# A fused GroupNorm and quantised 1x1 convolution: two channels of two conv groups in a partition, products as 64x64 quarters

## The reference, cut to what matters

```
v   = group_norm(x, 32 groups of 16 channels)            # eps 1e-5, no scale
xa  = round(clip((v - lA) / (uA - lA), 0, 1) * 15) / 15   # conv groups rotated: group g reads block g+1 of 4
wq  = (round(clip((w - lW) / (uW - lW), 0, 1) * 15) / 15 - 0.5) * 2
y   = grouped 1x1 conv(xa, wq)                            # 4 groups of 128 channels in, 128 out
y   = relu(y * inv + (beta - running_mean * inv))         # inv = gamma / sqrt(running_var + eps)
out = x + y + v
```

## Time and profile before

| | us |
|---|---|
| runs (three) | 258.25, 258.49, 258.49; median 258.49 |
| profiled execution | 258.41 |
| its span | 256.7 |
| VectorE busy | 230.0 |
| ScalarE busy | 215.2 |
| GpSimd busy | 212.0 |
| TensorE products and averages busy | 193.9 |
| mean granted TensorE clock | 0.902 |

### The profile page before, as it was taken

How to read it: one execution, slowest core, us unless ns; L and a number is a source line. 1 busy time by engine, 2 the same in 40 slices (tenths; PEclk the granted TensorE clock), 3 DMA queues, 4 the chain that set the end, 5 groups by cost and what they waited for, 6 DMA issues and landing times.

```text
span 256.7 us, 3463 instructions
## 1 busy us (share of the span) xinstructions
PE 193.9 (76%) x999; PEld 109.3 (43%) x999; DVE 230.0 (90%) x363; ACT 215.2 (84%) x394; POOL 212.0 (83%) x340
## 2 busy tenths in 40 slices
PE   1142996969889888979797997877696969889920
PEld 0132644435454444445443554343444435454510
DVE  2898698999999999999999899999999999969940
ACT  4437898999999999989999889999899888999300
POOL 6126869999999999999999999999999999999100
PEclk9999999797979798988979599999979797979995
DMA  6999999999999999999999999999999999999994
GB/s 225 398 411 411 408 409 406 418 416 417 418 414 418 417 416 418 411 418 416 416 415 416 418 416 413 419 417 415 417 413 418 416 418 409 402 400 402 393 399 193
DMA packets 34516, 103.25 MB, mean 402 GB/s; under 512 B 1202, under 2 KB 1730, under 8 KB 34498
## 3 DMA queue, kind: packets, MB, share of 16 engines
q1 hardware_dynamic: 18624, 54.86, 53.8%
q10 hardware_dynamic: 15874, 48.18, 47.0%
HBM read 51.65 MB, written 51.38 MB: 401 GB/s over the span
## 4 chain that ended last, share of the span: by engine, by line
POOL 52%; DVE 16%; issue 11%; PE 9%; ACT 5%; DMA 2%; DVEq 0%; SPq 0%; POOLq 0%; ACTq 0%
POOL images L413 27%; POOL levels L424 8%; DVE images L482 7%; PE prod L604 6%; DVE stats L460 4%; POOL dev L375 3%; DVE codes L475 3%; PE var_ps L584 3%; POOL dev L378 2%; DMA images<-in_x 2%; POOL scaled L404 2%; ACT levels L270 2%; POOL coef L406 2%; POOL norm L402 1%; ACT unused L242 1%
## 5 line engine op out<-in xcount | busy, mean ns | idle before, releaser
L604 PE MATMUL prod<-codes,w_t 128*128 128x392 bf16 x768 | 160.8, 369 | 7.9 <-DVE codes L475 2.9
L482 DVE SCALAR_TENSOR_TENSOR images<-prod,floor,images 128x784 f32<-128x784 f32 x128 | 128.0, 1019 | 8.5 <-PE prod L604 8.2
L413 POOL TENSOR_SCALAR images<-images,coef 128x784 f32<-128x784 f32 x120 | 123.7, 1042 | 0.0
L604 PEld LDWEIGHTS prod<-codes,w_t 128*128 128x128 bf16 x768 | 79.1, 110 | 81.6 <-issue 24.6
L270 ACT ACTIVATE levels<-images,coef 128x784 int16<-128x784 f32 x95 | 91.3, 1028 | 1.1 <-issue 1.1
L460 DVE BATCH_NORM_STATS2 stats<-images 128x6 f32<-128x392 f32 x136 | 68.9, 551 | 5.4 <-DMA images<-in_x 5.4
L236 ACT ACTIVATE unused<-images 128x784 bf16<-128x784 f32 x60 | 50.7, 847 | 7.5 <-DMA images<-in_x 5.2
L242 ACT ACTIVATE unused<-images,sums 128x784 bf16<-128x784 f32 x60 | 56.1, 939 | 0.1
L475 DVE TENSOR_SCALAR codes<-levels 128x3136 bf16<-128x3136 int16 x32 | 34.7, 1085 | 1.0 <-ACT levels L270 0.7
L584 PE MATMUL var_ps<-dev,avg 128*128 128x8 f32 x128 | 19.6, 280 | 20.0 <-POOL dev L382 20.0
L424 POOL TENSOR_SCALAR levels<-images,coef 128x784 int16<-128x784 f32 x33 | 33.6, 1020 | 0.1
(11 more groups left out here) (66 smaller groups left out, 83.2 us busy)
## 6 DMA issues: line engine op xcount, KB each, us to landing
images<-in_x SPq DMA_DIRECT2D x30, 1568.0 KB, 14.5
out<-images ACTq DMA_DIRECT2D x30, 1568.0 KB, 18.8
images<-in_x SPq DMA_DIRECT2D x8, 392.0 KB, 6.6
out<-images SPq DMA_DIRECT2D x1, 1568.0 KB, 8.8
out<-images SPq DMA_DIRECT2D x4, 392.0 KB, 7.4
w_raw<-in_weight SPq DMA_DIRECT2D x1, 256.0 KB, 6.5
rows<-in_channel_params ACTq DMA_DIRECT2D x1, 8.0 KB, 2.3
limit_row<-in_limits ACTq DMA_DIRECT2D x1, 0.0 KB
```

Of the source, the lines that this page charges most:

```text
L413: nc.gpsimd.tensor_scalar(here, here, coef[:, u % 2, 0, 1, G * j + o:G * j + o + 1], coef[:, u % 2, 1, 1, G * j + o:G * j + o + 1], ALU.mu ...
L482: nc.vector.scalar_tensor_tensor(out=two, in0=prod[:, k % SETS, :, 0:HALF], scalar=floor[:, o:o + 1], in1=two, op0=ALU.max, op1=ALU.add).t ...
L604: done = nc.tensor.matmul(prod[:, k % SETS, h, 0:HALF], w_t[:, part, output_group(g)], codes[:, n % 2, g, h * HALF:(h + 1) * HALF], start= ...
```

## The change

**Layout.** A partition now holds two neighbouring channels (2i, 2i + 1) of two conv groups: partitions 0 to 63 have blocks 0 and 3, partitions 64 to 127 have blocks 1 and 2. In HBM the two channels are one row of 6272 bytes. Slots 0 and 1 of a partition are the two channels (t = 0, 1) of its first block (y = 0), slots 2 and 3 those of its second (y = 1). Every load and every store becomes two DMAs, one for each half of the partitions; the increments they must reach double. ScalarE issues two DMAs for a store, SyncE two for a load. The four first pieces of images 0 and 1 become two pieces of two slots each, each of two DMAs.

**Products.** An image's 24 products of 128x128 become 96 of 64x64 by 392 columns (L685), four in turn on the four quarters of the array, each with its own weight load. They come as two halves of an image, t = 0 and t = 1, of 48 products that fill two of the three PSUM blocks at once, and `multiplied` rises once for a half. The wait for `final` and for `capped` stands at the start of each half. Ahead of a half, and again ahead of its last four products, stands a new product of the whole array with one column (`after_wait`, L657), which carries the waits for `final` and for the affine step.

**Order of finishing.** VectorE finishes slots in the order 0, 2, 1, 3 (`ORDER`); only F0 and F2 wait for TensorE. F3 now comes straight after F2, and the four halves of statistics stand behind it.

**Norm coefficients.** Both channels of a partition and slot pair are of one norm group, so the small tiles have half the width. The deviations are folded on GpSimd before TensorE's averages: two more GpSimd instructions for a pair (L434, L435), one more wait each. `sums` and the folded tile exist once instead of twice, so `sum_stats` and ScalarE's first sum of a pair now wait for the pair before. TensorE's average of squares moves from behind the means to the deviations.

**TensorE's program** is a loop of two images, run 14 times, with waits against registers, and three images behind it. `HELPED` falls from 4 to 3. At the start VectorE doubles the channel parameters (L556), and TensorE turns them twice.

```diff
+PSUM_SET = ((0, 1, 2, 0), (1, 2, 0, 1))
+ORDER = (0, 2, 1, 3)
+BODY = 2
...
+    LOW, HIGH = slice(0, HP), slice(HP, P)
+    GROUPS = ((LOW, slice(0, G, G - 1)), (HIGH, slice(1, G - 1)))
...
             def load(n):
                 j = n % RING
                 if n >= RING:
-                    sync.wait_ge(stored[j], DMA * (n // RING))
-                sync.dma_start(images[:, j], x_v[n]).then_inc(x_loaded[j], DMA)
...
+                    sync.wait_ge(stored[j], 2 * DMA * (n // RING))
+                for part, groups in GROUPS:
+                    sync.dma_start(pairs_of(images[part, j]),
+                                   x_v[n, groups].rearrange("y i f -> i y f")).then_inc(x_loaded[j], DMA)
...
+                folded(u, 2, nc.gpsimd.tensor_tensor(dev2[:], dev_, dev_, ALU.mult))
+                folded(u, 3, nc.gpsimd.tensor_tensor(dev2_half[:], dev2[:, :, 0:2], dev2[:, :, 2:4], ALU.add))
+                nc.gpsimd.tensor_tensor(dev2_sum[:].rearrange("p j g -> p (j g)"), dev2_half[:, :, 0], dev2_half[:, :, 1],
+                                        ALU.add).then_inc(dev_done, 1)
...
             def finish(n, g):
-                o = output_group(g)
-                k = G * n + g
-                dve.wait_ge(multiplied, k + 1)
+                o = ORDER[g]
+                if g % 2 == 0:
+                    dve.wait_ge(multiplied, 2 * n + g // 2 + 1)
...
                 finish(n, 2)
-                if m < B:
-                    half_stats(m, 0, 0)
                 finish(n, 3)
                 if m < B:
-                    half_stats(m, 0, 1)
-                    half_stats(m, 1, 0)
-                    half_stats(m, 1, 1)
+                    group_stats(m, 0)
+                    group_stats(m, 1)
...
+            def after_wait(out_set, h):
+                nc.tensor.matmul(prod[:, out_set, h, HALF:HALF + 1], w_t[:, 0, 0, 0], w_t[:, 0, 0, 0, 0:1], start=True, stop=True)
...
+            def multiply(trip, i, t):
+                n, sets = BODY * trip + i, PSUM_SET[i % 2][2 * t:2 * t + 2]
+                if t == 0:
                     pe.wait_ge(capped, n + 1)
...
+                if i > 0 or t == 1:
+                    pe.wait_ge(final, G * n + 1 if t == 1 else G * n - i % 2)
+                after_wait(sets[0], 0)
                 for part in range(PARTS):
...
+                    for s in range(2):
+                        for h in range(2):
+                            if (part, s, h) == (PARTS - 1, 1, 1):
+                                wait_affines(n, i, t)
+                                after_wait(sets[0], 0)
+                            for y, inputs in ((0, HIGH), (1, LOW)):
+                                for c, outputs in enumerate((LOW, HIGH)):
+                                    done = nc.tensor.matmul(prod[outputs, sets[y], h, 0:HALF], w_t[inputs, part, t, s, outputs],
+                                                            codes[inputs, i % 2, 2 * c + s, h * HALF:(h + 1) * HALF],
+                                                            start=(part == 0 and s == 0), stop=(part == PARTS - 1 and s == 1))
                 done.then_inc(multiplied, 1)
...
+            with pe.Fori(0, chained_images // BODY) as trip:
+                for i in range(1, 1 + BODY):
+                    image_products(trip, i, True)
```

311 lines of the change are left out of this document (174 added, 137 removed).

## The result

The changed kernel takes 357.3 us (median of four runs, 353.4 to 362.4) against 258.5 us, +99 us. The ratio is 1.358, with a 95% interval from 1.341 to 1.374; it compares fast executions alone (348.4 and 353.4 us, where four others took 357.0 to 364.0 at a lower granted clock), and by it the change costs 92 us, not 99. The direction was forecast, the size was not: +99 us stood against a forecast of +32, and the time lies outside the range of 264 to 335. The profiled execution has a span of 351.7 us, against 256.7.

A forecast was written before the change was run, and what follows sets the result against it. VectorE, ScalarE and GpSimd were taken as nearly full, DMA close behind; VectorE would now wait for TensorE. Last finish 246.9 + 23.6 + 11.9 + 2.0 = 284.4, span 288.8, plus 1.7: 290.5 us against 258.5; range 264 to 335.

The forecast's parts named there:

- T and the windows: T: end of the finish freeing a block to the finish using the half, 2.66 us; VectorE's windows: 1.85, 2.02, 3.04.
- The rivals in which issue binds or quarters run one after another: TensorE's quarter products: T = 6.0, 498 us; chance 0.09, shared with DMA at half rate throughout.
- The rival in which weight loads bind: TensorE's quarter weight loads set the pace: T 3.0 to 3.4, time 308 to 332 us; chance 0.19.
- Term 1: Images 0 to 26, 13.5 pairs: VectorE waits 1.75 us more in each pair for TensorE, +23.6 us.
- term 2: Last five images, 27 to 31, without statistics to fill the windows: 37.0 us instead of 25.1, +11.9.
- I price at 2.4: TensorE's clock: all work priced at 2.4 GHz; 3.6 us at 1.2 in each pair would cost up to +24 us.
- the text's signs of being wrong: F0 and F2 waiting under 10 us in all (mechanism); spacing of a group of four quarters not near 0.17 (T).
- term 5: TensorE's loop: register steps and a branch once a pair fall while TensorE waits for VectorE, 0 us; +14 if uncovered.
- term 3: Start: F0 of image 0 waits for 12 half-clock steps instead of 6; with first loads and parameters, +2.0 us in all.
- Its rival: Start: half-partition loads at half rate put the first F0 at 42.3, not 31: +11.3, time 302 us; chance 0.18.
- Term 4: GpSimd: two folds add 0.6 us to a pair's 13.9, covered by the 15.7 a pair then takes.
- Term 6: End: the last store lands unqueued, so the span ends 0.27 + 3.1 + 1.0 us after the last finish.

The follow-up runs named there:

- e12: e4 plus five unread 392-column products ahead of each half's wait, except at the second half of odd images: 276.3 us, 1.065 of the kernel before.
- e14: Changed kernel, loop written out, five unread products ahead of each half's wait except odd images' second half, and a fourth wait before the averages of means: 311.2 us.
- e4: The kernel before, whole-array products kept but released and awaited by halves of an image, with the changed kernel's waits and finishing order: 296.1 us, 1.141.
- e10: The kernel before with products released in halves of an image and every load and store as two 64-partition transfers: 318.2 us, 1.227.
- e18: e15 plus three more unread products ahead of the wait of the averages of means, loop kept: 312.2 us, 1.210.
- e1: Changed kernel with five unread products ahead of each half's wait from image 1 on, and a fourth wait before the averages of means: 324.8 us, 1.253.
- e8: Changed kernel with each one-column whole-array product issued twice in a row: 357.2 us, 1.369.
- e11: Changed kernel with TensorE's loop of two images written out, waits against constants, no register steps or branch: 325.3 us, 1.254.
- e16: e11 with two unneeded VectorE reductions ahead of each pair's sums, delaying the averages of means: 326.9 us, 1.263.
- e19: e11 with six unneeded VectorE reductions ahead of each pair's sums, delaying the averages of means: 369.8 us.
- e3: The kernel before with each load and store of an image issued as two 64-partition DMAs, nothing else changed: 296.3 us, 1.143.
- e2: Changed kernel with upper-half loads of images 0 to 5 issued from ScalarE's queue, so both partition halves move at once: 353.8 us.
- e15: Changed kernel, loop kept, with five unread products ahead of each half's wait except odd images' second half, and a fourth wait before the averages: 322.9 us.

## Why the prediction was wrong, and where it was right

**T and the windows were right.** At the full clock T is 2.65, against 2.66, and F1 and F3 never wait. Part of that match is luck: the two whole-array products cost 0.11 + 0.22 where 0.40 was forecast, the last group 0.36 where 0.33 was, the hand-overs 0.07 + 0.06 where 0.10 was. A group of four quarters takes (2.02 - 0.36) / 10 = 0.166 us, a row of four alone 0.36. The step from T = 2.26 to 2.66 was about right too: forecast at 19.8 us, and 18.6 from e12 to e14, of which the half transfers may be up to 5 (1.5 + 3.9 from e4 to e10). The rivals in which issue binds or quarters run one after another are out (a quarter every 0.04 us; their sum, by the way, comes to 496, not 498). The rival in which weight loads bind is out: the Trainium skill's "TensorEngine Tiling (Array Packing)", Restrictions, says that tiling by columns switches fast weight load off, but here 48 loads are hidden all the same. So is a price of 0.25 for each whole-array product, which the text took as better if the same page's drain on a change of mode (Key Properties) counts: 0.33 for the two, not 0.50. The mode's part in it no run separates.

**With the clock held up the sum holds, all but the start and the end.** In e18 (312.2 us, clock 0.991) the pair takes 16.2 us, against 14.1 + 1.75 = 15.85; the last five images take 37.3, against 37.0. Term 1 is then 28.0 in place of 23.6, term 2 12.2 in place of 11.9. The first finish comes at 43.72, 12.7 us later than forecast, and from the last finish to the end it is 8.1 us, 3.7 more. Added to the forecast's 290.5 these make the 311.8 us of e18's profiled execution to 0.2. What lies above that, up to 357.3, goes by the clock, as the 33 slow halves against e18's 2 show.

**Failed: "I price at 2.4".** The text had the price of a stretch of 3.6 us at 1.2 GHz in each pair, +24 us, but gave it no chance and no place in the range. The changed kernel spends 94 of 248 us at 1.2 GHz, some 7 us in each pair. That costs more than 1.8 a pair: 2.8, from e18's body (43.72 to 264.56 us) to the changed kernel's (42.39 to 300.67). From 357.3 down to e18's 312.2, the clock is worth 45 us (38 by the ratios), the loop's part in it included. Neither of the text's signs of being wrong looked at the clock, and neither fired: F0 and F2 wait 87 us, and the spacing is 0.166. The earlier trace rows had 0.87 in a kernel whose TensorE had slack to absorb it; e4 kept that kernel's mean clock, and there the clock cost 20 us. The change took the slack (TensorE and VectorE now work by turns, so a slow half is paid in full) and at the same time made TensorE stand still 1.15 us before most halves.

**Failed: term 5, "the register steps and the branch: 0".** The reasoning, they stand where TensorE waits anyway, is true of the halves. It is false of the averages, where two register waits stand behind the one that decides: they begin 0.23 us behind VectorE's `sums`, against 0.05 written out. By itself that is some 2 us over 14 pairs; by way of the clock the loop costs 32 (27 by the ratios). "If a branch costs 1 us, +14" was the wrong kind of risk.

**Failed: term 3, the start.** Its rival was right: first finish forecast at 42.3, measured 42.39. The last digit is luck, since e1, e8, e11, e14 to e16, e18 and e19, with the same transfers, have it at 42.9 to 43.7. I gave it 0.18. Its price, +11.3, was right for the start (11.6 from e4 to e10) and left out the end. The Trainium skill's "SBUF — State Buffer", Door 1, says that partitions 0 to 63 reach half of the ports. e3 shows 211 to 225 against 410 GB/s, in one direction only. I had a page against the change, no row for it, and 20 us of nothing but loads at the start; the edit itself turned every one of them into a half transfer. The likeliest start should have been this one.

**Term 4 right** as far as the traces show: the folds are covered. GpSimd is busy 217.3 us and waits 62.4 for ScalarE's `gmean`. **Term 6 wrong in size**: 8.1 us from the last finish to the end, where 4.4 were forecast. With whole stores it would have been right: e4 takes 3.5 there and e12 4.1. Stores in halves are slow when nothing is loaded (273 to 331 GB/s in e3), and e10 and e14, with half stores, take 8.7 and 8.2.

**The ledger** in medians: 258.5; halves of an image with transfers in halves 318.2; quarters and the rest of the change, without the loop, 325.3; with the loop 357.3. Its steps are no prices of single causes, since the clock moves in each (0.90, 0.88, 0.93, 0.83).

## What to carry to other kernels

When a change makes TensorE and its consumer take turns, price its work at both levels of the clock and let the range hold the slow one: here it was lost in the kernels whose TensorE stood still 1.1 to 1.2 us before most halves, was kept where that was filled, and every slow half was paid in full. If the trace after shows such stretches, fill the stand still with products that nobody reads, and try the places one by one; here three fillers at the averages, on top of those at the halves, gave back 11 us, while five more in VectorE's way (e1) gave back none. The mean clock does not tell the price: at 0.90 VectorE waited for TensorE 0.51 us a pair in the kernel before, and the same kernel in halves lost 20 us by it. Keep transfers on all 128 partitions where only loads or only stores run, above all ahead of the first result.

## What the hardware did that I had not expected

- Transfers of 64 partitions one behind another moved 211 to 225 GB/s when all were loads, 273 to 331 when all were stores, and 412 to 417 where loads and stores mixed (e3). Two queues on complementary halves, loads only, gave 294 at best (e2).
- TensorE at 1.2 GHz takes 3.81 us for 44 quarters, at 2.4 GHz 2.02. Most of the changed kernel's slow halves lie between (27 of 33, 2.58 to 3.75 us): the clock changed within them.
- A stand still that was 0.25 us longer, once in a pair (0.76 against 0.51), went with a mean clock of 0.83 instead of 0.93, and one of 0.99 with 0.80; one of 0.67 left it at 0.945. With fillers right behind the averages even 0.86 left the halves behind them at 2.4 GHz (e1).
- Waits against a register, with their register steps, each held back what followed by about 0.09 us when they stood behind the one that was released last: the means began 0.33 us behind `sums` with three of them (e15), 0.23 with two (the changed kernel), and 0.05 with the waits written out.
